# Down-stage LoRA and mix tables split once and kept in device memory, with the residual inside the mix weights

## The reference, cut to what matters

```python
def lora_add(base, inp, A, B):          # A, B of the sequence's adapter, rank 16
    t = einsum('bri,bni->bnr', A[idx], inp)
    return base + einsum('bor,bnr->bno', B[idx], t) * 0.5
gate = lora_add(x @ W_gate.T, x, A_gate, B_gate)      # 512 -> 1376
up   = lora_add(x @ W_up.T, x, A_up, B_up)
act  = silu(gate) * up
h    = x + lora_add(act @ W_down.T, act, A_down, B_down)   # 1376 -> 512
out  = h + einsum('bct,bcd->bdt', h, weights[condition])   # 32 x 32 per sequence
```

## Time and profile before

| | us |
|---|---|
| median of 3 runs | 447.93 (446.21 to 448.08) |
| profiled execution, its own time | 446.79 |
| its span | 445.0 |
| PE busy | 438.1 |
| DVE busy | 335.2 |
| ACT busy | 212.3 |
| POOL busy | 169.7 |

### The profile page before, as it was taken

The page is one execution under the profiler, slowest core; times in us unless marked ns, Lnnn a source line. Parts: engine busy times, 40 slices in busy tenths (PEclk is TensorE's granted clock), DMA queues, the critical chain, the costliest instruction groups (busy, mean ns, idle before and its releaser), DMA issues.

```text
span 445.0 us, 7248 instructions
## 1 busy us (share of the span) xinstructions
PE 438.1 (98%) x2475; PEld 393.5 (88%) x2475; DVE 335.2 (75%) x623; ACT 212.3 (48%) x397; POOL 169.7 (38%) x156
## 2 busy tenths in 40 slices
PE   8989999999999999999999999999999999999997
PEld 6877888888888888888888888999999999999996
DVE  6779999878867867857857858978667767766665
ACT  6746355366444544543543444843454454444531
POOL 2722223121121221121121452675776666756620
PEclk9999999999999999999999999999999999999999
DMA  8975664356555665665565599947776665556631
GB/s 243 381 242 146 181 172 114 109 172 188 145 181 151 159 172 145 161 173 144 159 173 144 145 287 340 247 138 202 215 201 208 208 180 178 177 178 196 191 96 47
DMA packets 99843, 81.12 MB, mean 182 GB/s; under 512 B 50944, under 2 KB 83200, under 8 KB 99808
## 3 DMA queue, kind: packets, MB, share of 16 engines
q1 hardware_dynamic: 88512, 47.27, 37.9%
q0 software_dynamic: 11008, 33.30, 24.8%
q10 hardware_dynamic: 288, 0.10, 0.1%
HBM read 65.18 MB, written 15.47 MB: 181 GB/s over the span
## 4 chain that ended last, share of the span: by engine, by line
PE 92%; DMA 2%; POOL 2%; issue 2%; DVE 1%; ACT 1%; SPq 0%; POOLq 0%
PE bank L1384 28%; PE bank L1262 9%; PE bank L1263 9%; PE bank L1261 9%; PE bank L1216 7%; PE bank L1217 7%; PE bank L1218 7%; PE bank L1283 4%; PE bank L1284 4%; PE bank L1414 2%; POOL a_raw L453 2%; PE bank L1394 2%; DMA b_raw<-in_b_rows,rows 2%; DMA gu_landing<-in_w_gate 1%; PE bank L1399 1%
## 5 line engine op out<-in xcount | busy, mean ns | idle before, releaser
L453 POOL DMA_INDIRECT b_raw<-in_b_rows,rows x48 | 51.8, 1078 | 188.7 <-DVE b_gu L803 188.1
L1384 PE MATMUL bank<-wd,actT_hi 128*128 128x288 f32 (+1 forms) x636 | 109.9, 295 | 0.0
L1384 PEld LDWEIGHTS bank<-wd,actT_hi 128*128 128x128 f32 (+1 forms) x636 | 93.8, 188 | 1.4 <-issue 0.2
L453 POOL DMA_INDIRECT a_dn_raw<-in_a_dn_rows,rows x64 | 77.3, 1208 | 19.5 <-issue 19.5
L803 DVE SCALAR_TENSOR_TENSOR b_gu<-b_raw,low_rows,b_gu 128x1024 fp32r<-128x1024 f32 (+1 forms) x48 | 55.6, 1159 | 26.8 <-ACT b_gu L513 26.8
L1384 PE MATMUL bank<-wd,actT_lo 128*128 128x288 f32 (+1 forms) x318 | 68.1, 296 | 0.0
L513 ACT ACTIVATE b_gu<-b_raw 128x1024 fp32r<-128x1024 f32 (+1 forms) x48 | 46.2, 963 | 11.2 <-DMA b_raw<-in_b_rows,rows 9.8
L1384 PEld LDWEIGHTS bank<-wd,actT_lo 128*128 128x128 f32 (+1 forms) x318 | 51.0, 188 | 0.0
L603 ACT ACTIVATE act<-bank 128x512 f32<-128x512 f32 (+1 forms) x48 | 26.1, 546 | 41.4 <-PE bank L1284 41.4
L910 DVE TENSOR_TENSOR act<-act,bank 128x512 f32<-128x512 f32 (+1 forms) x48 | 29.8, 621 | 8.6 <-PE bank L1284 7.8
L799 DVE TENSOR_TENSOR actT_lo<-actT_raw,actT_hi 128x1280 fp32r<-128x1280 f32 (+1 forms) x32 | 27.0, 886 | 11.6 <-ACT actT_hi L513 11.6
(11 more groups left out here) (180 smaller groups left out, 1004.2 us busy)
## 6 DMA issues: line engine op xcount, KB each, us to landing
actT_raw<-actT_dram SPq DMA_DIRECT2D x16, 640.0 KB
actT_dram<-staging SPq DMA_DIRECT2D x64, 128.0 KB, 2.9
x_sb<-in_x SPq DMA_DIRECT2D x16, 256.0 KB, 2.9
xT_raw<-in_xT SPq DMA_DIRECT2D x15, 256.0 KB, 2.7
out<-out_sb SPq DMA_DIRECT2D x15, 256.0 KB
a_raw<-in_a_gu_rows SPq DMA_DIRECT2D x56, 64.0 KB, 2.7
actT_dram<-staging SPq DMA_DIRECT2D x32, 88.0 KB, 3.2
wd_raw<-in_w_down SPq DMA_DIRECT2D x10, 256.0 KB, 5.9
```

The source lines that it names most:

```text
L453: return pool.indirect_dma_start(dst, None, src, bass.IndirectOffsetOnAxis(ap=rows[:, tile, col:col + 1], axis=0))
L1384: last = pe.matmul(ps_down[e][half][:, 0:HALF], a[e][0:n, c, :], wd[0:n, c, part, at:at + HALF], start=(c == 0 and i == 0), stop=(c == NC ...
```

## The change

All 16 adapters' A and B of the down matrix and all 16 mixing matrices are split once, in the gate and up stage, in seven **rounds**: four of A (4 adapters each, 128x704), two of B (128x512), one of the mix (128x128), to which DVE first adds the identity. SP loads a round into `a_dn_raw[0]`; ACT writes the high half to `a_dn_raw[1]`; DVE writes the low half over the raw rows; SP stores both halves to tables in device memory; the next round is loaded once they have landed. Rounds 0 and 1 stand in pair 3, 2 and 3 in pair 4, 4 and 5 in pair 5, 6 in pair 6.

In the down stage POOL gathers A (both halves, rows of 1408 bytes in place of 704; from tile 2 on) and B (low or high row by partition, straight into the matmul's operand) from the tables. ACT copies both halves of A into `wd`; the splits of B and mix and DVE's low half of A are gone. SP loads the mixing matrices itself, in 4 loads per tile, each with a row number that it reads first (`load_mix`), straight into the diagonal blocks. Since the identity is in the mix, the residual sum after it is gone, and ACT copies the bank out (`copy_out`). The mask's sign is turned to +0.5 for the low rows before the first tile. The last tile keeps the old path for the mix.

```diff
...
+A_ROUNDS = ADAPTERS // TILE_SEQS
+ROUNDS = A_ROUNDS + 3
+FIRST_ROUNDS = 3
...
+    a_table = nc.dram_tensor("a_table", (ADAPTERS * P, 2 * A_DN), F32, kind="Internal").ap()
+    b_table = nc.dram_tensor("b_table", (2 * ADAPTERS * RANK, H), F32, kind="Internal").ap()
+    mix_table = nc.dram_tensor("mix_table", (ADAPTERS * CH, 2 * CH), F32, kind="Internal").ap()
...
+        with ExitStack() as then:
+            a_pair = [sb(f"a_pair{e}", [P, TILE_SEQS, 2 * A_DN], F32, then) for e in range(2)]
...
-        mix_raw = [sb(f"mix_raw{e}", [P, CH]) for e in range(2)]
-        mix_hi = sb("mix_hi", [P, P], F32R)
-        mix_lo = sb("mix_lo", [P, P], F32R)
+        mix_raw = sb("mix_raw", [P, CH])
+        mix_w = [sb(f"mix_w{e}", [P, 2, P], F32R) for e in range(2)]
...
-        b_dn_raw = [sb(f"b_dn_raw{e}", [P, H]) for e in range(2)]
+        b_dn = [sb(f"b_dn{e}", [P, H], F32R) for e in range(2)]
...
+        def a_round(i):
+            return a_dn_rows[TILE_SEQS * i * P:TILE_SEQS * (i + 1) * P, :].rearrange("(a p) n -> p a n", p=P)
+        def table_parts(i):
+            if i < A_ROUNDS:
+                raw, to = slice(0, TILE_SEQS * A_DN), slice(TILE_SEQS * i * P, TILE_SEQS * (i + 1) * P)
+                return raw, [a_table[to, part * A_DN:(part + 1) * A_DN].rearrange("(a p) n -> p a n", p=P)
+                             for part in range(2)]
+            if i < A_ROUNDS + 2:
+                r0 = (i - A_ROUNDS) * P
+                return slice(0, H), [b_table[part * ADAPTERS * RANK + r0:part * ADAPTERS * RANK + r0 + P, :]
+                                     for part in range(2)]
+            return slice(0, TILE_SEQS * CH), [mix_table[:, part * CH:(part + 1) * CH]
+                                              .rearrange("(a p) n -> p a n", p=P) for part in range(2)]
+        def table_sb(e, cols, n=None):
+            flat = a_dn_raw[e][:, :, :].rearrange("p q n -> p (q n)")[:, cols]
+            return flat if n is None else flat.rearrange("p (a n) -> p a n", n=n)
+        def rounds_of(pr):
+            return [i for i in (2 * (pr - FIRST_ROUNDS), 2 * (pr - FIRST_ROUNDS) + 1) if 0 <= i < ROUNDS]
...
+            def load_round(i):
+                reached(sp, tables_stored, 32 * i)
+                if i < A_ROUNDS:
+                    sp.dma_start(a_dn_raw[0][:, :, :], a_round(i)).then_inc(table_landed, 16)
+                elif i < A_ROUNDS + 2:
+                    r0 = (i - A_ROUNDS) * P
+                    sp.dma_start(table_sb(0, slice(0, H)), b_dn_rows[r0:r0 + P, :]).then_inc(table_landed, 16)
+                else:
+                    sp.dma_start(table_sb(0, slice(0, TILE_SEQS * CH), CH),
+                                 mix_rows.rearrange("(a p) n -> p a n", p=P)).then_inc(table_landed, 16)
+                    sp.dma_start(table_sb(0, slice(TILE_SEQS * CH, (TILE_SEQS + 1) * CH)), eye)\
+                        .then_inc(table_landed, 16)
+            def store_round(i):
+                cols, tables = table_parts(i)
+                n = A_DN if i < A_ROUNDS else H if i < A_ROUNDS + 2 else CH
+                sp.wait_ge(table_ready, i + 1)
+                for part, to in enumerate(tables):
+                    src = table_sb(1 - part, cols, n if len(to.shape) == 3 else None)
+                    sp.dma_start(to, src).then_inc(tables_stored, 16)
+            def load_mix(m, e):
+                reached(sp, mix_done, 2 * (m - 1))
+                for q in range(TILE_SEQS):
+                    r = slice(q * CH, (q + 1) * CH)
+                    col = 2 * TILE_SEQS + 2
+                    row = sp.value_load(rows[q * CH:q * CH + 1, m, col:col + 1], min_val=0, max_val=(ADAPTERS - 1) * CH)
+                    sp.dma_start(mix_w[e][r, :, r].bitcast(F32),
+                                 mix_table[bass.ds(row, CH), :].rearrange("c (h n) -> c h n", h=2))\
+                        .then_inc(mix_landed[e], 16)
...
+                rounds = rounds_of(pr)
...
                     load_a(pr + 1, 1)
+                if rounds:
+                    load_round(rounds[0])
                 for s in range(2):
                     if last and s == 0:
                         load_down()
...
                         sp.wait_ge(p6_done, 2 * FAST)
                         load_actT(1, 1)
                     spill(pr, s)
+                    if s < len(rounds):
+                        store_round(rounds[s])
+                    if s + 1 < len(rounds):
+                        load_round(rounds[s + 1])
...
             load_actT(2, 0)
+            sp.wait_ge(tables_stored, 32 * ROUNDS)
+            load_mix(0, 0)
             load_x(1, 1)
             load_actT(3, 1)
+            load_mix(1, 1)
             store(0, 0)
             spill(PAIRS - 1, 2)
             load_x(2, 0)
+            load_mix(2, 0)
             for j in range(1, TILES // 2 - 1):
                 load_actT(2 * j + 2, 0)
                 store(2 * j - 1, 1)
                 load_x(2 * j + 1, 1)
+                load_mix(2 * j + 1, 1)
                 load_actT(2 * j + 3, 1)
                 store(2 * j, 0)
                 load_x(2 * j + 2, 0)
+                load_mix(2 * j + 2, 0)
...
             def gather_a_dn(m, q0=0, q1=TILE_SEQS):
-                reached(pool, a_dn_ready, m - 1)
+                if m == 0 and q0 == 0:
+                    pool.wait_ge(tables_stored, 32 * ROUNDS)
+                if m == 2:
+                    for t in range(2):
+                        pool.wait_ge(section_done[t], NS * PAIRS)
+                reached(pool, a_dn_copied, m - 3)
                 for q in range(q0, q1):
-                    gather(a_dn_raw[m % 2][:, q, :], a_dn_rows, m, TILE_SEQS + 1 + q).then_inc(a_dn_landed[m % 2], 16)
+                    to, table = (a_dn_raw, a_dn_rows) if m < 2 else (a_pair, a_table)
+                    gather(to[m % 2][:, q, :], table, m, TILE_SEQS + 1 + q).then_inc(a_dn_landed[m % 2], 16)
...
             def gather_b_dn(m):
-                reached(pool, b_dn_ready, m - 1)
-                gather(b_dn_raw[m % 2][:, :], b_dn_rows, m, 2 * TILE_SEQS + 1).then_inc(b_dn_landed[m % 2], 16)
-
-            def gather_mix(m):
-                reached(pool, mix_ready, m - 1)
-                gather(mix_raw[m % 2][:, :], mix_rows, m, 2 * TILE_SEQS + 2).then_inc(mix_landed[m % 2], 16)
+                reached(pool, down_lora_done, 2 * (m - 1))
+                gather(b_dn[m % 2][:, :].bitcast(F32), b_table, m, 2 * TILE_SEQS + 1).then_inc(b_dn_landed[m % 2], 16)
...
-            gather_mix(0)
+            gather(mix_raw[:, :], mix_rows, TILES - 1, 2 * TILE_SEQS + 2).then_inc(last_mix_landed, 16)
             pool.wait_ge(s_used, FAST)
             gather_b_dn(0)
+            gather_b_dn(1)
             for m in range(2, TILES):
                 gather_a_dn(m)
-                pool.wait_ge(down_done, m - 1)
-                gather_b_dn(m - 1)
-                gather_mix(m - 1)
-            gather_b_dn(TILES - 1)
-            gather_mix(TILES - 1)
+                gather_b_dn(m)
...
+            def split_round(i):
+                if i < ROUNDS - 1:
+                    sc.wait_ge(table_landed, 16 * (i + 1))
+                else:
+                    sc.wait_ge(table_mix_added, 1)
+                cols, _ = table_parts(i)
+                hi(table_sb(1, cols).bitcast(F32R), table_sb(0, cols)).then_inc(table_hi_ready, 1)
...
                     split_down(0, 3)
+                for i in rounds_of(pr)[0:1]:
+                    split_round(i)
...
                 split_b(pr, 2, 1)
+                for i in rounds_of(pr)[1:2]:
+                    split_round(i)
...
             def split_a_dn(m, e):
                 sc.wait_ge(a_dn_landed[e], nth(64, m, e))
                 reached(sc, down_done, m - 1)
-                hi(wd_a(0, e), a_dn_raw[e][:, :, :].rearrange("p q (c r) -> p q c r", c=NC)).then_inc(a_dn_hi_ready, 1)
+                if m < 2:
+                    hi(wd_a(0, e), a_dn_raw[e][:, :, :].rearrange("p q (c r) -> p q c r", c=NC))\
+                        .then_inc(a_dn_hi_ready, 1)
+                else:
+                    for part in range(2):
+                        of = a_pair[e][:, :, part * A_DN:(part + 1) * A_DN]
+                        last = hi(wd_a(part, e), of.rearrange("p q (c r) -> p q c r", c=NC))
+                    last.then_inc(a_dn_copied, 1)
...
-            def split_mix(m, e):
-                sc.wait_ge(mix_landed[e], nth(16, m, e))
-                reached(sc, mix_done, 2 * m)
-                for q in range(TILE_SEQS):
-                    r = slice(q * CH, (q + 1) * CH)
-                    last = hi(mix_hi[r, r], mix_raw[e][r, :])
-                last.then_inc(mix_hi_ready, 1)
...
-            def split_b_dn(m, e):
-                sc.wait_ge(b_dn_landed[e], nth(16, m, e))
-                reached(sc, down_lora_done, 2 * m)
-                hi(b_dn[:, :], b_dn_raw[e][:, :]).then_inc(b_dn_hi_ready, 1)
+            def copy_out(m, e):
```

(47 more changed lines are left out.)

89 lines of the change are left out of this document (38 added, 51 removed).

## The result

The changed kernel takes 466.91 us (median of 4 runs, 464.77 to 469.88) against 447.72 for the kernel before on the same chip: a ratio of 1.044, 95% interval 1.038 to 1.050. The forecast was 455.4, range 448.5 to 462.0. The sign was right; the loss is 19.2 us where I had 7.5, and the time lies 4.9 us above the range. The profiled execution took 469.88 us with a span of 468.1, against 445.0 before: 23.1 us to find. It is the slowest of the four, some 3 us above their median.

What follows compares the result with a forecast made beforehand. PE (TensorE) was taken as the bound, busy all of the time in both stages. 7.6 + 0.5 = 8.1 us on the profiled 446.79 gave 454.9; half the 1.1 us offset to the runs' median made it 455.4, range 448.5 to 462.

Steps and rivals of the forecast that it cites:

- What is taken away is worth nothing: Down stage: splits and sums leave ACT and DVE, but no PE wait ends in them, so PE gains 0.
- The second round of pairs 3, 4 and 5: Gate stage, pair ends: stores 4.4 us, then load 3.2, delay DVE's sum; PE waits 3.1, 3.1 and 1.4, sum 7.6.
- Pair 6 costs 0 to 0.5: Gate stage: one round, of the mix, delays splits by some 0.8 us, just under 0.9 slack; taken as 0, at most 0.5.
- SP's four loads: Down stage: addressed mix loads take SP about 4.0 us per tile, fit the 9.93 us tile, and cost 0.
- Start of the down stage: Tile 2: the last gather of A comes later, into the activations' burst; PE loses 0 to 1.5 us, taken as 0.5.
- Rival (b): Down stage starves for late A gathers, deciding at a landing 3.3 us into the tile; 12 tiles add 10 us; chance 0.12.
- My own terms: Down-stage tile: copies 1.5 us, h 1.2 and its low half 0.4 must end by PE's mix, 6.1 us in.
- The turns between queues: Down-stage DMA: packet-by-packet turns would keep a burst from holding gathers back; one gather's 5.92 us was held against even turns.
- My own sign of being wrong: Wrong if PE shows no wait between 110 and 250 us, no pair grows longer, or the time comes from the down stage.

Runs made afterwards that it cites:

- all_holds: Changed kernel with mid-pair rounds, padding, A gathered first, mix loads behind activations, and POOL's A gathers held on every tile from 3 on: 449.92 us, ratio 1.0066.
- rounds_only: The kernel before plus the seven table rounds, tables written but not read, old down stage: 456.36 us, ratio 1.019.
- mid_pair: Changed kernel with one round of a pair moved to its middle and loads issued half a pair ahead of their split: 461.36 us, ratio 1.030.
- act_first: Changed kernel with SyncE's four mix loads behind the load of the activations, in the steady down stage: 464.57 us, ratio 1.033.
- run 6: Changed kernel gathering 704-byte A rows from the input: 462.68 us, ratio 1.028. Reservation: a kernel with unedited down stage also showed only 3.2 us of mix waits.
- a_first: Also run 4: changed kernel with POOL gathering A of tile m ahead of B of tile m-1: 459.78 us, ratio 1.027.
- run 3: Also `aligned`: changed kernel with 1,152 unused bytes per partition more, so later buffers are moved by 2,048: 469.41 us, ratio 1.043.
- shifted: The kernel before with an unused buffer of 896 bytes per partition, placing later buffers as in the changed kernel: 451.0 us, ratio 1.0076.
- run 1: Same run as `rounds_only`: the kernel before plus the seven table rounds and nothing else: 456.36 us, ratio 1.019.

## Why the prediction was right in sign and too small

- **What is taken away is worth nothing:** right. DVE's busy time fell from 335.2 to 298.6 us, and even `all_holds`, with nearly every new wait gone, is not faster: PE's products are the same and already stood end to end.
- **The second round of pairs 3, 4 and 5, 7.6 us:** right in place, in chain and in size. 6.5 us in the changed kernel and 7.5 in `rounds_only`; gone with either of two ways to load earlier. Two of its parts were off against each other: I had 4.4 for the stores and 3.2 for the load, and measured 3.8 and 4.5. By the Trainium skill (DMA: Bandwidth & Descriptors, section Anatomy of one DMA) they would be 3.65 and 2.83 us as an estimate. The store agrees, the load does not, here with 352 KB that land in 4.9 us in the median; but the page gives its fit for DMAs that GpSimd issues, and these are SyncE's. Pair 5, with rounds of B, cost 0.5 and not 1.4 (1.05 in `rounds_only`).
- **Pair 6 costs 0 to 0.5:** right in itself, there is no gap in it or at its end. The gap of 0.43 us in pair 7 (1.3 in `rounds_only`, none in `mid_pair`) was not in the forecast; it goes with the rounds, and its path was not traced.
- **SP's four loads, 4.0 us per tile, "needed a tile or more later. I take 0":** the size was 5.05 us, and the conclusion was wrong. I asked whether SP's own loads come in time, and not what moves behind them. Ahead of the activations they push 0.7 MB into the gathers of A; sent behind them, in `act_first`, 5.1 us of the waits went (with the reservation of run 6).
- **Start of the down stage, 0.5 (0 to 1.5):** too small, 2.35 us, by the chain that I had written: the last gather of A, issued at 305.2, reaches ACT at 311.2, and the low half of the activations, on which PE waits, ends at 315.7. How much of it is bytes, order or burst is open: it was 1.3 in `a_first`, but also in `act_first`, which edits nothing there.
- **Rival (b), which the sum took at 0 with a chance of 0.12, is the step that failed; the waits for the mix cost 7.9 us.** I wrote its chain down with its point of decision, a landing 3.3 us into the tile, and expected 1.5 to 3. The chain above gives, for the tile that began at 325.8 (331.77 plus the usual distance, less the 6.1 us up to the mix), a landing at 331.25, 5.4 us in: 2.1 late, which is the 2.09 that PE waited. The last gather is issued at 325.49, 0.3 us ahead of the tile, and needs 5.76 us to land, where my 1.5 to 3 left it 1.8 to 3.3. I sized it as if the queues were nearly free, while the spills had already landed after up to 9.0 us. It struck in five tiles and not twelve, 7.9 us for my 10. My own terms (1.5, 1.2 and 0.4 off 6.1) put the point of decision at 3.0, not 3.3; in the chain above the 2.74 us from landing to product make it 3.4. A term that is decided at, or 0.3 us beyond, its own bound deserves more than 0.12.
- **The turns between queues:** the Trainium skill (the same page, section Queues, rings and completion order) speaks of turns packet by packet. Here a gather of A took 5.76 us under a burst and the waits shrank when the burst was moved: whatever the turns are, they did not protect the gathers. The 5.92 us that I held against even turns are no evidence, though. They are POOL's own time and not a landing: in every one of the 20 profiled kernels one gather near there, the 67th or 68th of the program, takes 5.9 or 6.7 us, and it is 5.92 in the kernel before, where the queues are at 0.21 in its last 2 us, as in the changed one, where they are at 0.99 and 0.53.
- **Not in the forecast at all:** the pace of the 512-column products (3.6 us of the span, though in run 3 larger waits took its place) and the half clock in the ramp (1.6 us at 32 us, of which 0.9 is left at 40; `shifted` and `aligned` have it too).
- **My own sign of being wrong**, that the time comes from the down stage, came true for 10 of the 23 us.

Rounds 8.3 us (run 1, measured alone) and the down stage's order on POOL 7.5 us (1.044 less 1.027 of 448, run 4) are the two large parts of the 19.2.

## What to carry to other kernels

When an instruction is put ahead of others on a DMA-issuing engine, price what moves behind it, and on which transfers that falls: the loads themselves came in time here, the burst that they delayed fell on the gathers. A round trip through device memory inside a hand-ordered list costs its landing times wherever one buffer serves two rounds, here 8.3 us for seven rounds of at most 0.36 MB; half a pair of distance or a second buffer hides it, but for 0.3 us. Causes that sit in one chain don't add, and those that hide behind each other reappear: after each remedy read the waits anew.
